# Attention scores split into a rounded rectified part and a gathered linear part

## The reference

```python
x = x * jax.lax.rsqrt(ms + EPS) * rms_w
x = x @ W_down
xl = (x @ Wl).reshape(n, H, D)
xr = (x @ Wr).reshape(n, H, D)
msg = xl[src] + xr[dst]
act = jnp.where(msg > 0, msg, NEG_SLOPE * msg)
e = jnp.einsum('ehd,hd->eh', act, att)
m = jax.ops.segment_max(e, dst, num_segments=n)
p = jnp.exp(e - m[dst])
denom = jax.ops.segment_sum(p, dst, num_segments=n)
alpha = p / (denom[dst] + 1e-16)
out = jax.ops.segment_sum(alpha[..., None] * xl[src], dst, num_segments=n)
return out.reshape(n, HID) @ W_up
```

## Time and profile before

| what | us |
| --- | --- |
| median of three runs | 1489.52 |
| the three runs | 1489.06, 1491.56, 1489.52 |
| the profiled execution, its own time | 1491.28 |
| span of the profiled execution | 1489.5 |
| PE busy | 1410.9 (95%) |
| PEld busy | 1144.6 (77%) |
| DVE busy | 781.9 (52%) |
| ACT busy | 424.5 (29%) |
| POOL busy | 255.5 (17%) |

### The profile page before, as it was taken

One profiled execution on the slowest core, in us unless ns is written; L12 is line 12 of the kernel. 1 busy time (PEld: TensorE's weight loads), 2 busy tenths in 40 slices (PEclk: granted clock), 3 DMA queues, 4 the chain that ended last, 5 costly groups with the idle time before them and its releaser, 6 DMA issues.

```text
span 1489.5 us, 17808 instructions
## 1 busy us (share of the span) xinstructions
PE 1410.9 (95%) x6845; PEld 1144.6 (77%) x6845; DVE 781.9 (52%) x1359; ACT 424.5 (29%) x716; POOL 255.5 (17%) x307
## 2 busy tenths in 40 slices
PE   3888999959999999899999999999999999999997
PEld 3886888836666666678888888888888888888886
DVE  6996777538888888645346621410133332410244
ACT  7862323246666664212111100201200000210000
POOL 3000000057777673100000000000010100000000
PEclk9997999979999999999999999999999999999999
DMA  1666344456556652432127443230066544400253
GB/s 48 188 181 207 107 106 140 96 161 212 167 167 172 208 170 70 144 121 95 54 92 248 157 182 116 90 114 0 1 217 221 183 130 142 159 1 0 78 191 128
DMA packets 102404, 195.97 MB, mean 132 GB/s; under 512 B 27143, under 2 KB 61752, under 8 KB 102320
## 3 DMA queue, kind: packets, MB, share of 16 engines
q1 hardware_dynamic: 77866, 121.28, 27.2%
q0 software_dynamic: 22640, 73.09, 14.2%
q10 hardware_dynamic: 1814, 0.47, 0.2%
HBM read 140.87 MB, written 53.92 MB: 131 GB/s over the span
## 4 chain that ended last, share of the span: by engine, by line
PE 57%; DVE 1%; DMA 0%; DVEq 0%; issue 0%; ACT 0%; POOL 0%
PE layers_y_ps L1946 35%; PE layers_y_ps L1967 18%; PE layers_turn_ps L1930 2%; PE layers_up_ps L1913 1%; PE layers_y_ps L1983 1%; DMA x_d<-fetched_x 0%; DVE layers_w_lo L2102 0%; DVE layers_y L2146 0%; PE layers_y_ps L1991 0%; DVE layers_y L605 0%; DVE layers_ln_stats L599 0%; PE layers_turn_ps L1901 0%; DVE layers_parts_lo L2119 0%; DVEq L600 0%; PE layers_y_ps L1901 0%
## 5 line engine op out<-in xcount | busy, mean ns | idle before, releaser
L517 POOL DMA_INDIRECT attention_got<-xl_d,heads_first_src x156 | 162.1, 1039 | 61.6 <-issue 43.8
L1967 PE MATMUL layers_y_ps<-layers_parts_hi,layers_counts 128*128 128x512 f32 x464 | 143.0, 389 | 0.0
L1967 PE MATMUL layers_y_ps<-layers_parts_lo,layers_counts 128*128 128x512 f32 x464 | 142.9, 389 | 0.0
L1946 PE MATMUL layers_y_ps<-layers_w_hi,layers_parts_hi 128*128 128x512 f32 x400 | 125.4, 395 | 0.0
L1946 PE MATMUL layers_y_ps<-layers_w_lo,layers_parts_hi 128*128 128x512 f32 x400 | 123.3, 389 | 0.0
L1946 PE MATMUL layers_y_ps<-layers_w_hi,layers_parts_lo 128*128 128x512 f32 x400 | 123.2, 389 | 0.0
L1967 PEld LDWEIGHTS layers_y_ps<-layers_parts_lo,layers_counts 128*128 128x128 f32 x464 | 87.1, 188 | 18.1
L1967 PEld LDWEIGHTS layers_y_ps<-layers_parts_hi,layers_counts 128*128 128x128 f32 x464 | 86.9, 188 | 17.9
L2119 DVE SCALAR_TENSOR_TENSOR layers_parts_lo<-layers_y_ps,layers_parts_hi 128x1024 fp32r<-128x1024 f32 x16 | 19.6, 1225 | 144.7 <-ACT layers_parts_hi L2062 144.7
L1334 PE MATMUL attention_row_ps<-attention_bent,edges_att_rows 128*128 128x512 f32 x184 | 95.4, 601 | 0.0
L1367 PE MATMUL attention_mix_ps<-attention_weighted,attention_hot 128*110 128x260 f32 x368 | 95.1, 382 | 0.0
(11 more groups left out here) (338 smaller groups left out, 2792.1 us busy)
## 6 DMA issues: line engine op xcount, KB each, us to landing
layers_counts<-counts_d SPq DMA_DIRECT2D x30, 640.0 KB, 4.0
layers_rest<-x_d SPq DMA_DIRECT2D x23, 512.0 KB, 3.9
self_d<-layers_y POOLq DMA_DIRECT2D x20, 512.0 KB, 5.6
x_d<-layers_y POOLq DMA_DIRECT2D x19, 512.0 KB, 2.9
fetched_x<-x_d SPq DMA_DIRECT2D x17, 512.0 KB, 3.6
fetched_raw<-in_L_gnn_W_self POOLq DMA_DIRECT2D x16, 512.0 KB, 5.7
fetched_raw<-in_L_gnn_W_neigh POOLq DMA_DIRECT2D x16, 512.0 KB, 8.9
heads_dst_wide<-in_dst_held SPq DMA_DIRECT2D x13, 512.0 KB, 4.6
```

The costliest lines, as they stand in the source:

```text
L517: nc.gpsimd.indirect_dma_start(got[:, t, :], None, xl_d, bass.IndirectOffsetOnAxis(src[:, a * QUAD + t:a * QUAD + t + 1], 0))\
L1946: last = nc.tensor.matmul(y_ps[n % 2][:, a:a + HALF], rows_in[t][:, k * P:(k + 1) * P], w[k][:, a:a + HALF], start=(k == 0 and p == 0), st ...
L1967: last = nc.tensor.matmul(y_ps[n % 2][:, a:a + HALF], counts[c % 2][:, k, :], part[k][:, a:a + HALF], start=(k == 0 and part is hi), stop= ...
```

## The change

The larger of m and 0.2 m is 0.2 m + 0.8 relu(m). The score is therefore a linear part, which depends on the source's row and the destination's row alone, and a product of 0.8 att with relu(m). Within one destination a constant drops out of the softmax, so of the linear part only the source's share is kept.

*The linear part.* `project_scores` makes 0.2 times Wl att for each head, four columns that `left` gets behind its 256; the left product is 272 columns wide (XL_ROW = HID + LINE, 12 of them zero), and so are the rows of `xl_d` and of the gather (1088 bytes). It runs on DVE after `add_bias(0)` and ahead of the loop over tiles. ScalarE splits `left` and `right` once it is done. In a visit, ScalarE copies the four columns of each half into `linear` (`take_linear`), and PE transposes them into `row_ps` (`turn_linear`), where the scores are added.

*The rectified part.* ScalarE writes the rounded relu (`bent_hi`), DVE the rest (`bent_lo`), and a score is two rounded products. `att_rows` holds 0.8 att, its high part in some columns and its low part in others, so that a window of 128 columns gives both, and the low one lands in rows of its own. `pick` and `fold` add the two again: `turn` is no longer a transpose but a product with `fold` in full float32, 8 columns wide.

*The division.* ScalarE does it for the first 21 visits (`divide`), at q = 0 of the visit j + 4; DVE stops behind the reciprocal, and waits at the next visit until the division has been done. `shifted_rows` is now kept in a buffer of `far`, and `nothing` in `linear`.

```diff
+XL_ROW = HID + LINE
...
-        left = WeightSplit(m, "left", io["L1_gnn_Wl"], HID, blocks=KH)
+        left = WeightSplit(m, "left", io["L1_gnn_Wl"], XL_ROW, blocks=KH)
...
-                product(nc, xl_ps, dt_hi, dt_lo, left, width=HID)
+                product(nc, xl_ps, dt_hi, dt_lo, left, width=XL_ROW)
...
-                    for split in (w, left, right):
+                    w.high(act, nc)
+                    act.wait_ge(s["linear_made"], 1)
+                    for split in (left, right):
                         split.high(act, nc)
...
+            def project_scores():
+                dve.wait_ge(s["att_ready"], 16)
+                for k in range(KH):
+                    dve.wait_ge(left.raw_ready[k], 16)
+                    nc.vector.scalar_tensor_tensor(out=loop_sum[:, :], in0=left.raw[:, k, 0:HID], scalar=SLOPE,
+                                                   in1=att_row[:, :], op0=ALU.mult, op1=ALU.mult)
+                    dve.drain()
+                    last = nc.vector.tensor_reduce(left.raw[:, k, HID:HID + HEADS],
+                                                   loop_sum[:, :].rearrange("p (h d) -> p h d", h=HEADS), AX.X, ALU.add)
+                    dve.drain()
+                last.then_inc(s["linear_made"], 1)
...
             add_bias(0)
+            project_scores()
             for tile in range(BLOCKS + 2):
...
+    DIVIDED_BY_ACT = SUBS - 2
...
-        got = [first_got] + slots("got", [P, QUAD, HID], F32, GOT - 1)
+        got = [first_got] + slots("got", [P, QUAD, XL_ROW], F32, GOT - 1)
...
+            def turn_linear(j):
+                pe.wait_ge(linear_ready, QUADS * (j + 1))
+                for t in range(QUAD):
+                    nc.tensor.matmul(row_ps[j % 2][:, t * P:(t + 1) * P], linear[:, t, :], g["ident"][:, :],
+                                     is_transpose=True, start=(t == 0), stop=False, skip_group_check=True)
...
-                nc.tensor.matmul(row_ps[j % 2][:, :], g["att_rows"][:, k, (1 - a) * HEADS:(1 - a) * HEADS + P],
-                                 bent[i % 3][:, :], start=(i % UNITS == 0), stop=(i % UNITS == UNITS - 1),
-                                 skip_group_check=True).then_inc(scored, 1)
+                for part in (bent_hi, bent_lo):
+                    last = nc.tensor.matmul(row_ps[j % 2][:, :], g["att_rows"][:, k, (1 - a) * HEADS:(1 - a) * HEADS + P],
+                                            part[i % len(part)][:, :], start=False,
+                                            stop=(i % UNITS == UNITS - 1 and part is bent_lo), skip_group_check=True)
+                last.then_inc(scored, 1)
...
-                    last = nc.tensor.matmul(row_ps[j % 2][:, t * P:(t + 1) * P], shifted_rows[:, t * P:(t + 1) * P],
-                                            g["ident"][:, :], is_transpose=True, start=(t == 0),
+                    last = nc.tensor.matmul(row_ps[j % 2][:, t * P:t * P + QUADS * HEADS],
+                                            shifted_rows(j)[:, t * P:(t + 1) * P], g["fold"][:, :], start=(t == 0),
                                             stop=(t == QUAD - 1), skip_group_check=True)
...
+                if q == 2 and i < LAST:
+                    turn_linear(j)
                 if 2 <= i < LAST + 2:
                     score(i - 2)
...
-                nc.scalar.activation(scaled[i % 2][:, :], message_ps[i % 2][:, :], ACT.Copy, scale=SLOPE)\
-                    .then_inc(scaled_ready, 1)
+                nc.scalar.activation(bent_hi[i % 3][:, :], message_ps[i % 2][:, :], ACT.Relu).then_inc(high_ready, 1)
+
+            def take_linear(j, a):
+                act.wait_ge(*gathered(j, a))
+                nc.scalar.activation(linear[:, :, a * HEADS:(a + 1) * HEADS], held(j, a)[:, :, HID:HID + HEADS],
+                                     ACT.Copy).then_inc(linear_ready, 1)
...
+            def divide(j):
+                b = j % 2
+                act.wait_ge(inverted, j + 1)
+                if j >= 2:
+                    act.wait_ge(mixed_stored[b], 16 * (j // 2))
+                for h in range(HEADS):
+                    last = nc.scalar.activation(mixed[b][:, h * HEAD_DIM:(h + 1) * HEAD_DIM],
+                                                summed[0:SUB, j, h, 0:HEAD_DIM], ACT.Copy, scale=inverse[:, h:h + 1])
+                last.then_inc(out_ready, 1)
...
+                if q == 0 and i < LAST:
+                    if j == 0:
+                        act.wait_ge(linear_cleared, 1)
+                    take_linear(j, 0)
                 if q == 0 and 2 <= j <= SUBS + 1:
                     keep_sums(j - 2)
+                if q == 0 and 4 <= j < DIVIDED_BY_ACT + 4:
+                    divide(j - 4)
                 if q == 0 and j in SPLIT_VISITS:
                     high(SPLIT_VISITS.index(j))
                 if q == 1 and 1 <= j <= SUBS:
                     take_rows(j - 1)
+                if q == 1 and i < LAST:
+                    take_linear(j, 1)
...
-                dve.wait_ge(scaled_ready, i + 1)
-                nc.vector.tensor_tensor(bent[i % 3][:, :], message_ps[i % 2][:, :], scaled[i % 2][:, :], ALU.max)\
+                dve.wait_ge(high_ready, i + 1)
+                if i >= 2:
+                    dve.wait_ge(scored, i - 1)
+                nc.vector.scalar_tensor_tensor(out=bent_lo[i % 2][:, :], in0=message_ps[i % 2][:, :], scalar=0.0,
+                                               in1=bent_hi[i % 3][:, :].bitcast(F32), op0=ALU.max, op1=ALU.subtract)\
                     .then_inc(bent_ready, 1)
...
                 dve.wait_ge(summed_up, j + 1)
+                if 1 <= j <= DIVIDED_BY_ACT:
+                    dve.wait_ge(out_ready, j)
...
-                if j >= 2:
-                    dve.wait_ge(mixed_stored[b], 16 * (j // 2))
+                if j < DIVIDED_BY_ACT:
+                    return
+                dve.wait_ge(mixed_stored[b], 16 * (j // 2))
                 nc.vector.tensor_tensor(mixed[b][:, :].rearrange("p (h d) -> p h d", h=HEADS), whole[:, :, 0:HEAD_DIM],
```

More of the change, by code:

```diff
@@ L853, in _ @@
                     pe.wait_ge(s["xl_ready"], CLEAR)
[L854 removed]
+                    nc.tensor.matmul(most_t, most[:, :], g["ident"][:, 0:HALF - XL_ROW - P], start=True, stop=True)\
                         .then_inc(s["most_turned"], 1)
@@ L996, in take_heads @@
                 dve.wait_ge(s["xl_ready"], tile + 1)
-                nc.vector.tensor_tensor(loop_sum[:, :], xr_ps[:, :], xl[:, u, :], ALU.add)\
+                linear = xl[:, u, HID:HID + HEADS]
+                nc.vector.tensor_tensor(loop_sum[:, :], xr_ps[:, :], xl[:, u, 0:HID], ALU.add)\
                     .then_inc(s["xr_ready"], 1)
                 dve.drain()
-                nc.vector.scalar_tensor_tensor(out=loop_sum[:, :], in0=loop_sum[:, :], scalar=SLOPE,
-                                               in1=loop_sum[:, :], op0=ALU.mult, op1=ALU.max)
+                nc.vector.tensor_scalar(loop_sum[:, :], loop_sum[:, :], 0.0, 1.0 - SLOPE, ALU.max, ALU.mult)
                 dve.drain()
```

84 lines of the change are left out of this document (52 added, 32 removed).

## The result

The changed kernel takes 1494.66 us, the median of seven runs (1493.45 to 1496.48), the kernel before in the same comparison 1489.68. The ratio is 1.0026, with a 95% interval of 1.0014 to 1.0037: **slower by a quarter of a per cent**, where faster was forecast, and outside the range of 1480 to 1492.

What follows compares the result with a forecast made beforehand. DVE's loop was taken to set ten visits and PE nine. Terms of -3.4 - 2.3 - 1.2 + 1.35 + 1.3 + 0.5 + 0.15 = -3.6 us on the 1489.52 median gave 1486.0 us, range 1480 to 1492.

Steps and rivals of the forecast that it cites:

- it would end near 460.0, the spread starts at 460.32: Split visits: despite about 1.0 us more ScalarE work, its rows finish before the spread; cost 0, upper end +0.34 each.
- the spread waits for ScalarE's rows: Sign in the attention visits that the forecast is wrong; no size given.
- ScalarE becomes the bound: Rival: in split visits ScalarE's queue passes the point where the spread waits; the 3.4 gain goes, 1489.4 us, chance 0.14.
- I take +0.28 on what waits for it: Visits without a split: the eight-column turn delays the clamp by 0.28 us; 11.35 us a visit, -2.3 us over nine.
- What is late next is turn: Visits without a split: after the change the clamp waits for turn; bounds 11.07 to 11.51 us a visit.
- The next two visits already wait on turn: 0.: The two visits after the first, half-clock one: no change in time, 0 us.
- In the last ones the same wait eats the divide: 0: Last visits of the attention loop: the wait on turn cancels the gain from moving the divide, 0 us.
- Visit 0: First visit, at half the clock: half of each score's time goes, against four slow transposes; -1.2 us (0 to -2).
- DVE's own saving: Attention loop: the divide leaves DVE, -0.34 us; split visits go from 11.93 to 11.59, -3.4 us over ten.
- The front: Front stage: project_scores delays tile 0's sum, +1.35 us; PE's clock falls, +1.3; wider left product +0.4, stage end 0.1.
- The gather rival: Rival: 1088-byte rows lengthen POOL's gather issues by a sixth, making the gather the bound; 1495.0 us, chance 0.11.
- The rule that speaks against the move: Attention loop: multiplies, maxima and relu belong on VectorE; divide kept there, the -3.4 would be 0, the sum 1489.4.

Runs made afterwards that it cites:

- the kernel with the later store: Changed kernel with ScalarE's division moved to the end of its visit and the store one load later in SyncE's order; 1492.83 us, ratio 1.0023.
- the short turn: Changed kernel with turn as four transposes again, leaving out the low part of the attention vector; 1488.62 us, ratio 0.9992.

## Why the prediction was wrong

- **ScalarE, "it would end near 460.0, the spread starts at 460.32 [...] I take 0 and keep +0.34 a split visit as upper end (the gain is eaten)".** This step failed. The place was the right one: the spread waits for ScalarE's rows, which the prediction named as a sign of being wrong. The margin of some 0.2 us was not there. From the start of the exponentials to the end of the rows the forecast has 3.77 us (456.23 to 460.0); measured are 4.47 (484.54 to 489.01). The division was nearly right (1.06 us, 1.0 estimated). Put at nothing was the wait of the first relu for its message, 0.64 (485.44); in the visit of the earlier trace rows it was 0. PE makes that message behind turn, and the clamp now follows turn closely. So the spread is some 0.3 to 0.4 us late, and the stretch behind the clamp is 0.46 to 0.55 longer in ten visits (5.21 to 5.30, once 5.12, against 4.75): some 5 of the 6.6 us. The rival "ScalarE becomes the bound" had this mechanism, and capped its price at the gain of 3.4.
- **Turn, "I take +0.28 on what waits for it".** The duration grew by 0.35, but from turn's start to the clamp it is 1.06 us (483.25 to 484.31), not 0.64 + 0.28. With the forecast's upper end, 0.44, the visit with no split comes to 11.51; 11.53 was measured (6.77 + 4.76), 11.35 forecast: nine times 0.18, 1.6 us. "What is late next is turn" was right.
- **"The next two visits already wait on turn: 0."** Where the clock held (the kernel with the later store), visit 1 takes 11.10 (10.87 before) and visit 2 11.46 (11.61 before), so 0 was near. The 2.2 us of the table are nearly all the fall of the clock in visit 1, for which the forecast had no term, and whose cause stays open. "In the last ones the same wait eats the divide: 0" cost 0.6: 28.46 with the short turn alone, 29.10 as changed.
- **Visit 0** gave 0.4 of the 1.2 us. The two profiles before differ there by 1.0, so that its term was wrong isn't shown.
- **DVE's own saving** was right: 7.20 to 6.85 from maximum to clamp, and clamp to maximum 4.75 where nothing is late. With the waits gone the split visits are 11.61, as forecast (11.59).
- **The front** was right in its mechanism, and in its sum partly by luck. Counted from its first product, which itself starts between 127.69 and 130.17 us, the first message comes 189.0 us later before and 192.6 changed (means of two and three profiles): +3.6, where 3.15 was set without the setup. The fall of the clock cost some 0.95 us (14.80 from the second sum to the third, 13.85 where the clock held), with 1.3 set. But the nine tiles behind the first sum take 146.0 us even where the clock held, and 144.6 before: 1.4, with 0.4 set for the wider product. That product grew as reckoned (281 to 288 ns a matmul); what makes the rest isn't shown.
- **The gather rival** gave the nearest number, 1495.0, by luck: an issue takes 949 ns in the median (946 before), and its rows land after 3.2 us (3.4 before). The beats that the Trainium skill counts for rows which don't start on 256 bytes ("DMA: Bandwidth & Descriptors", section "How a descriptor splits into AXI transactions") leave no mark in these medians.
- **The rule that speaks against the move** (the Trainium skill, "ScalarE: Activation LUTs", section "Rules for kernel authors") agrees with the trace on the speed, 1.06 us on ScalarE against 0.42 on VectorE. By the traces it was right for the place where the division stood: VectorE did it in 2 us less over nineteen visits. It was wrong for the place at the end of the visit, where ScalarE idled and the three visits fell to 34.75 us.

## What to carry to other kernels

When work is moved to an engine with idle time, list every instruction behind it in that engine's queue and ask who waits for each; the idle time counts only where it lies. A margin of 0.2 us read in the old trace need not be there in the new one: go through the queue again from its first wait, since the change also moves what that wait is for. Where an operation is already waited for, its growth is paid in full, and a narrow product in full float32 is not a small one: here the weights were loaded all the same, eight loads of 192 ns for eight columns each. When two engines are near the bound, a saving on both turns the loop into a chain of waits, and the order in the queues sets its length.

## What the runs showed that I had not expected

- A store that waits for a late result holds back index loads behind it on the same queue: 33 us from one step moved by half a visit, and all of it gone with the store one load later.
- Idle pieces of PE of 1.10, 1.12 and 0.69 us, the first of them a wait for a gather, stood ahead of the fall of the clock to 0.50 in visit 1. They don't decide it: with the short turn it stayed at 1.00 behind pieces of 1.18, 1.14 and 0.69, and in one profile of the late division it fell with no first piece at all.
- Gains shown in the trace ahead of the layers reached the timed runs in part only: the late division's 5.4 us came out as 4.6 in the spans of three profiles each, as some 3 us in the medians of all executions, on different chips (1492.97 of 13 against 1495.94 of 9), and as 0.5 us in the ratios (1.0023 against 1.0026). What makes the rest is open.
